# Summing products ahead of the transposes with accumulating transfers in a two-layer convolution kernel

## The reference

```python
enh  = dw_conv3x3(conv1x1(x))                      # one filter per channel
h1, h2 = split(group_conv3x3(x))
attn = conv1x1(h1 * h2) * attgamma + conv1x1(x)    # 16 values per pixel
attk = attn^T @ selfw                              # per pixel, per group of 2 channels: 2 x (2*9) weights
y    = einsum('bpgij,bpgj->bpgi', attk, uf)        # uf: the 3x3 surroundings of enh, in groups of 2 channels
out  = (y + attn^T @ selfb) * ga1 + enh + x
```

## Time and profile before

| | |
|---|---|
| median of 3 runs | 5735.58 us (5731.08 to 5740.74) |
| the profiled execution | 5731.75 us, its span 5730.0 us |
| busy in the span | PE 97%, PEld 72%, DVE 89%, ACT 60%, POOL 73% |
| layer 0 | about the first 1860 us |
| layer 1 | the rest, 64 bands |
| HBM traffic | 62 GB/s over the span |

### The profile page before, as it was taken

One profiled execution on the slowest core, in us unless ns is written; L12 is line 12 of the kernel. 1 busy time (PEld: TensorE's weight loads), 2 busy tenths in 40 slices (PEclk: granted clock), 3 DMA queues, 4 the chain that ended last, 5 costly groups with the idle time before them and its releaser, 6 DMA issues.

```text
span 5730.0 us, 115887 instructions
## 1 busy us (share of the span) xinstructions
PE 5581.3 (97%) x39944; PEld 4131.5 (72%) x39944; DVE 5083.3 (89%) x5319; ACT 3463.1 (60%) x4284; POOL 4185.7 (73%) x1831
## 2 busy tenths in 40 slices
PE   8999999999998699999999999999999999999998
PEld 7888888888886366666666766666666666766666
DVE  7888888888887789999899998989999899998989
ACT  6888888888886455455554555555455554555553
POOL 4565555555654678888888888888888888888885
PEclk9999999999999799999999999999999999999999
DMA  2222222222221222222222222222222222222221
GB/s 89 73 73 73 73 73 77 77 73 73 73 73 62 52 72 67 69 64 65 73 67 70 62 65 71 67 71 66 68 64 65 73 67 70 62 65 71 67 71 45
DMA packets 155248, 394.20 MB, mean 69 GB/s; under 512 B 35136, under 2 KB 38400, under 8 KB 155136
## 3 DMA queue, kind: packets, MB, share of 16 engines
q1 hardware_dynamic: 154800, 392.87, 22.0%
q10 hardware_dynamic: 400, 0.69, 0.1%
HBM read 219.37 MB, written 136.31 MB: 62 GB/s over the span
## 4 chain that ended last, share of the span: by engine, by line
PE 54%; DMA 8%; DVE 3%; SPq 1%; issue 1%; ACT 1%; DVEq 0%; POOLq 0%; POOL 0%; ACTq 0%
PE ps_t L888 18%; PE ps_k L871 17%; DMA xin<-layer_out 8%; PE ps_m L854 8%; PE ps_p L840 5%; PE ps_t L905 2%; DVE products L1100 2%; PE ps_t L896 1%; PE ps_t L903 1%; PE ps_m L861 1%; ACT out_sb L991 1%; SPq L736 1%; DVE products L1062 0%; SPq L684 0%; SPq L711 0%
## 5 line engine op out<-in xcount | busy, mean ns | idle before, releaser
L805 POOL TENSOR_TENSOR enh<-enh,tap 128x1280 f32<-128x1280 f32 (+1 forms) x1024 | 2512.9, 2454 | 485.2 <-ACT tap L1009 431.7
L1100 DVE TENSOR_TENSOR products<-ps_k,enh 128x1024 f32<-128x1024 f32 x1792 | 2157.4, 1221 | 269.4 <-PE ps_k L871 248.5
L871 PE MATMUL ps_k<-att,basis 128*128 128x512 f32 x4608 | 1719.3, 459 | 22.1 <-DVE products L1100 10.9
L1009 ACT ACTIVATE tap<-e,dw 128x1280 f32<-128x1280 f32 (+1 forms) x1024 | 1260.6, 1251 | 0.0
L871 PEld LDWEIGHTS ps_k<-att,basis 128*128 128x128 f32 x4608 | 719.4, 190 | 701.2 <-DVE products L1100 451.1
L296 POOL TENSOR_TENSOR hidden_lo<-hidden,hidden_hi 128x1024 fp32r<-128x1024 f32 x256 | 693.1, 2726 | 717.2 <-DVE hidden_hi L501 717.2
L888 PE MATMUL ps_t<-ident_swap,products 128*128 128x128 f32 x6144 | 921.7, 273 | 0.0
L888 PE MATMUL ps_t<-ident,products 128*128 128x128 f32 x6144 | 919.7, 272 | 0.2 <-POOL products L811 0.2
L888 PEld LDWEIGHTS ps_t<-ident,products 128*128 128x128 f32 x6144 | 757.3, 140 | 175.7 <-POOL products L811 0.5
L811 POOL TENSOR_TENSOR products<-products 128x1024 f32<-128x1024 f32 x256 | 611.8, 2390 | 268.0 <-DVE products L1100 268.0
L888 PEld LDWEIGHTS ps_t<-ident_swap,products 128*128 128x128 f32 x6144 | 719.9, 141 | 0.0
(11 more groups left out here) (111 smaller groups left out, 7378.1 us busy)
## 6 DMA issues: line engine op xcount, KB each, us to landing
xin<-layer_out SPq DMA_DIRECT2D x64, 1280.0 KB, 7.2
xt<-in_x SPq DMA_DIRECT2D x128, 512.0 KB, 4.0
layer_out<-xo SPq DMA_DIRECT2D x128, 512.0 KB, 2.9
x_own<-layer_out SPq DMA_DIRECT2D x128, 512.0 KB, 4.0
out<-out_sb SPq DMA_DIRECT2D x256, 256.0 KB, 2.0
att<-att_hi SPq DMA_DIRECT2D x512, 32.0 KB, 1.9
att<-att_lo SPq DMA_DIRECT2D x512, 32.0 KB, 2.0
h_up<-h_sb SPq DMA_DIRECT2D x256, 16.0 KB
```

The costliest lines, as they stand in the source:

```text
L805: nc.gpsimd.tensor_tensor(own, own, tap_sb[add % TAP_BUFFERS][:, 0:hi - lo, :], ALU.add).then_inc(dw_done, 1)
L871: mm = nc.tensor.matmul(ps_k[KERNEL_BUFFER[q]][:, BANK * s:BANK * (s + 1)], basis[:, 2 * t + s, :], att[p][:, j, :], start=True, stop=True)
L1009: nc.scalar.activation(tap_sb[add % TAP_BUFFERS][:, 0:hi - lo, :], src, ACT.Copy, scale=dw[:, t:t + 1]).then_inc(tap_ready, 1)
L1100: nc.vector.tensor_tensor(out, kernels, enh[p][:, r:r + CHUNK_ROWS, dx:dx + W].unsqueeze(1).to_broadcast([C, 2, CHUNK_ROWS, W]), ALU.mult) ...
```

## The change

Twelve of the 36 products were summed into their neighbours before; now it is twenty. The 28 stored products of a band make 16 terms instead of 24. The 20 sums are 8 on VectorE, 2 on GpSimd and 10 as DMA transfers with an add at the destination, which GpSimd issues: `merge_by_dma` waits for product q + 1 and adds place q + 1 to place q. Each has a semaphore of its own, for which TensorE waits ahead of the term, and VectorE before it writes the source's place again. Four sums are of three products (4+5+6, 13+14+15, 22+23+24, 31+32+33): VectorE adds the first two, a transfer the third. Terms, taps, convolution, back and the rest get other slots.

```diff
-VECTOR_MERGES = (0, 3, 10, 12, 18, 21, 27, 30)
-POOL_MERGES = (6, 15, 24, 33)
+VECTOR_MERGES = (4, 7, 13, 16, 22, 25, 31, 34)
+POOL_MERGES = (11, 29)
+DMA_MERGES = (0, 2, 5, 9, 14, 18, 20, 23, 27, 32)
+SUMMED_BEFORE = tuple(sorted(POOL_MERGES + DMA_MERGES))
-TERMS = [q for q in STORED if q - 1 not in POOL_MERGES]
+TERMS = [q for q in STORED if q - 1 not in SUMMED_BEFORE]
-TERM_SLOT = {1: 4, 2: 5, 4: 11, 5: 9, 6: 15, 8: 12, 9: 13, 11: 18, 13: 19, 14: 20, 15: 26, 17: 23, 19: 26, 20: 27, 22: 34, 23: 33, 24: 35, 26: 36, 28: 37, 29: 39, 31: 41, 32: 42, 33: 48, 35: 45}
+TERM_SLOT = {0: 10, 2: 14, 5: 15, 8: 13, 9: 21, 11: 20, 14: 27, 17: 26, 18: 34, 20: 32, 23: 35, 26: 36, 27: 40, 29: 48, 32: 49, 35: 47}
-BACK_SLOTS = [21, 30, 38, 54]
+BACK_SLOTS = [19, 28, 38, 53]
-POOL_MERGE_PLACES = (2.1, 4.5, 10.5, 13.45)
-TAP_PLACES = ((0.6000000000000001, 4.5, 5.0, 9.5, 14.5, 18.0, 18.5, 18.5, 20.5), (23.5, 25.0, 27.0, 30.0, 34.5, 35.5, 36.5, 38.5, 43.0))
-CLEAR_PLACES = (35, 53)
-H_PROD_SLOT = 27
-ATT_HIGH = 29
-ATT_LOW = 32
-CONV_SLOTS = [33, 33, 40, 40, 43, 43, 43, 43, 50, 50, 52, 52, 56, 56, 59, 59, 62, 62]
-COEFFICIENT_SLOT = 28
+POOL_MERGE_PLACES = (4.1, 13.5)
+DMA_MERGE_PLACES = (1.1, 0.5, 2.5, 3.9000000000000004, 7.5, 7.9, 8.7, 10.5, 12.4, 14.1)
+TAP_PLACES = ((0.0, 0.0, 0.0, 0.0, 6.0, 9.0, 9.5, 10.0, 11.0), (21.0, 21.5, 25.5, 27.0, 31.5, 32.0, 33.5, 35.0, 41.0))
+CLEAR_PLACES = (34, 60)
+H_PROD_SLOT = 25
+ATT_HIGH = 28
+ATT_LOW = 33
+CONV_SLOTS = [33, 33, 40, 40, 43, 43, 45, 45, 51, 51, 52, 52, 55, 55, 56, 56, 63, 63]
+COEFFICIENT_SLOT = 26
...
+                def merge_by_dma(n, index):
+                    q = DMA_MERGES[index]
+                    pool.wait_ge(product_ready, SLOTS_IN_BAND * n + OP_COUNT["product", q + 1])
+                    pool.sem_inc(dma_merge_begun, 1)
+                    nc.gpsimd.dma_start(products[:, PLACE[q], :, :], products[:, PLACE[q + 1], :, :],
+                                        accum_op=ALU.add).then_inc(dma_merged[q], 16)
...
+                    elif q in DMA_MERGES:
+                        pe.wait_ge(dma_merged[q], 16 * n + 16)
...
+                    elif at - 1 in DMA_MERGES:
+                        at_least(dve, dma_merged[at - 1], 16 * before + 16)
```

More of the change, by code:

```diff
@@ L657, in convolve @@
         pool_merged, pool_term_done = sem("pool_merged"), sem("pool_term_done")
+        dma_merge_begun = sem("dma_merge_begun")
+        dma_merged = {q: sem(f"dma_merged{q}") for q in DMA_MERGES}
         sum_done, sumT_ready, back_done, out_ready = sem("sum_done"), sem("sumT_ready"), sem("back_done"), sem("out_ready")
@@ L811, in merge @@
                     nc.gpsimd.tensor_tensor(lead, lead, products[:, PLACE[q + 1], :, :], ALU.add).then_inc(pool_merged, 1)
+                def merge_by_dma(n, index):
[4 more added lines that the diff above has]
+                                        accum_op=ALU.add).then_inc(dma_merged[q], 16)
                 ORDER = ([(t - 1, add_tap, 1, (0, t)) for t in range(1, TAPS)] +
                          [(TAPS - 1 + t - 1, add_tap, 1, (1, t)) for t in range(1, TAPS)] +
-                         [(place, merge, 2, (i,)) for i, place in enumerate(POOL_MERGE_PLACES)])
+                         [(place, merge, 2, (i,)) for i, place in enumerate(POOL_MERGE_PLACES)] +
+                         [(place, merge_by_dma, 2, (i,)) for i, place in enumerate(DMA_MERGE_PLACES)])
                 def step(items, p):
@@ L820, in step @@
                         if items[k] is not None:
-                            if action is merge:
+                            if action in (merge, merge_by_dma):
                                 action(items[k], *args)
```

## The result

The changed kernel takes 5727.19 us (median of 20 runs, 5714.12 to 5741.81), the kernel before 5740.02 us (20 runs): ratio 0.9978, 95% interval 0.9971 to 0.9985. That is 13 us less where 205 were forecast, 0.2 us a band. The profiled execution took 5723.56 us with a span of 5721.8.

A forecast was written before the change was run, and what follows sets the result against it. TensorE was taken as the bound. VectorE's 53.9 + 1.2 for late sums gave 55.1 us, GpSimd's 55.1 + 1 gave 56.1 us a band; 3.2 us less times 64 is 205 us, so 5530 us, range 5410 to 5800.

The forecast's parts named there:

- The bound before: Kernel before, convolution stage: TensorE's instruction stream bounds the 59.3 us band, VectorE 5 us behind.
- The issue: Accumulating transfer's issue in GpSimd's in-order stream: 1.1 us each, scaled from xin's 0.73, bounds 0.33 and 2.39.
- GpSimd's stream: GpSimd per band: adds 39.3 us, two merges 4.8, ten issues 11.0, together 55.1 us, more than VectorE.
- The times of the sums against TensorE's slots: Landings of transferred sums: (0,1) 1.2 us late for TensorE, (14,15) 0.9 late, (27,28) just in time.
- Other queues: SP's queue: xin's load has 7.6 us for 7.2, free unless sharing engines with an accumulating transfer, then one to three us.
- rival B: Accumulating transfers crowd the loads or land at 6 us and more: 58.5 us a band, 5680 us; chance 0.16.
- the load of h_up: From h_rows to h_prod: 7.6 us available for 5.4 us of issues, landing and h_sb, hidden with 2 us to spare.
- if the sums cost nothing: Band with fewer terms and free sums: 54.5 us, as VectorE and TensorE, coupled by two kernel buffers, won't mesh perfectly.
- TensorE's stream: Eight terms fewer a band at 0.88 us: 7.0 us less, from 58.8 to 51.8 us.
- A: Rival: GpSimd's issue is cheap, 0.5 us or less; VectorE bounds the band at 54.5 us, 5425 us; chance 0.20.
- C: Rival: an issue costs GpSimd over 1.5 us, so GpSimd paces the band; 5880 us at 1.75 us; chance 0.15.
- D: Rival: transfers each hold all DMA engines over 4.6 us and bound the band; 6290 us at 5.5 us; chance 0.09.

The follow-up runs named there:

- one attempt at it: Changed kernel with the xin load first, plus convolution moved from slots 40 and 63 to 41 and 62, product 17's term from 26 to 23: 5559.79 us.

## Why the prediction was wrong

**The bound before and the new prices were right.** The issue was forecast at 1.1 us and took 1.015; GpSimd's stream at 55.1 us a band came to about 52 (887 of 1000 us busy), mostly because an add starts 0.6 us behind an issue and only grows by some 0.35. The landing was forecast at 5 us and took 5.2, the share at 0.5 to 0.85 and came to 0.70. The times of the sums against TensorE's slots were close enough: with everything else in place (the load first), TensorE's weight loads wait 25 times in some 53 bands, 0.4 us each, and its matmuls 1.6 us in all. The Trainium skill (Collectives: The Full Stack, The bandwidth ceiling, under Why ReduceScatter is half of AllGather) states that the add in such a transfer costs time through its second source read and not in itself. The runs here agree: the transfers' own queue takes 23.4% of the engines' time in the stage when plain and 46.5% with the add.

**The step that failed is "Other queues".** It found the right place: xin's load, issued behind store(o,3), with 7.6 us for 7.2, and "one to three us a band if it does" share the engines. But the forecast then took the case in which it doesn't, and gave the other to rival B with 0.16. The same working had the engines 30 to 47 us busy in a band of 55; with a cover of 0.4 us, sharing was the rule and not the exception. The time from xin's issue to TensorE's need was as forecast, 7.6 to 7.9 us in the two bands shown (7.6); the term that was off is the landing, 9.4 us for 7.2, and the wait, 1.66 us for none. The run with the load first takes away that wait, and with it the lowered clock and the wait for h_up, and gives 5560 us; the run with an eighth of the bytes gives 5556 in the original order. Rival B was the mechanism, and its price, 58.5 us a band, was 0.6 us short of 59.07.

**What B's price left out.** No row of the kernel before had shown TensorE idle for 2.5 us in the stage, and the prediction priced a wait by its length. Behind 18 of the 25 long waits the clock fell, worth 0.6 us a band on the average. And the load of h_up, named in the prediction and put as hidden with 2 us to spare, cost VectorE 0.4 us a band (19.0 us in 50.8 bands, 18 times). B's 2 to 3 us over the forecast came out at 3.0, but mostly as these three together and not as one wait.

**A second error didn't show.** The prediction put the band at 54.5 us if the sums cost nothing; without transfers it is 56.08. TensorE's stream was put at 51.8 us, and its busy time there is 53.8 us a band (2875.86 of 3000 us), 4.8 less than before and not 7.0, with 2.3 us idle. A term does still take 0.88 us by its starts, and the modelled ends of TensorE's records reach into gaps, so how much of the difference is work and how much is gaps isn't shown. The meshing with VectorE, put at 0.6 us over 53.9, costs 2 us. By taking away one load at a time, ten issues from GpSimd or 7 us from VectorE, the band stays at 56.0 to 56.1 us; what is left as the bound is TensorE with its order of work, by exclusion. The forecast of 56.1 us came from GpSimd's sum, which doesn't bind. Had xin been in time, it would have been nearly right (56.3), by luck and for the wrong engine. Which order of TensorE's work would close the last 2 us stays open; one attempt at it gained nothing.

**The rivals.** A (cheap issue) is refuted by the 1.015 us, and its time wouldn't have come either: with plain issues of 0.56 us the kernel takes 5588 us, without any 5539, not 5425. C isn't what happened, ten issues leave GpSimd 4 us of slack; that GpSimd paces the band when its stream is long enough is shown by the halved transfers, its deciding point of 1.5 us an issue by no run. D is refuted: the ten hold the engines for 0.46 x 59.1 / 10 = 2.7 us each, not 4.6.

## What to carry to other kernels

When an edit adds traffic, take every transfer whose landing an engine meets with less than a transfer's worth of cover and price it as late; then look at what its issue is queued behind, since moving it ahead of an unrelated store was worth 167 us here, with no instruction more. Test an added mechanism in parts: the issue with few of the bytes, the bytes without the add, neither. Take away what seems to bind before calling it the bound. And price a wait of TensorE by its length and by the clock that can fall behind it.

## What the runs showed of the hardware

An accumulating transfer between two places of SBUF, 128 rows of 4 KB, takes GpSimd 1.02 us for the issue against 0.56 us for the plain one (1.07 us at an eighth of the bytes), and lands in 5.2 us against 3.3. With two issues in a row, of half the bytes each, the records overlap and are 1.54 us long on the average, 1.1 us of busy time each. The add behind an issue starts 0.6 us after the issue's start and is some 0.3 us longer behind an accumulating one. A 1280 KB load landed in 7.3 us without the transfers, in 8.3 beside plain ones and in 9.4 beside accumulating ones.

The granted clock fell to 0.54 behind a wait of 2.47 us and came back some 4 us after. In the changed kernel it fell behind 18 of the 25 waits of 2.10 to 2.89 us, the shortest of them 2.24, and behind none of the 25 of up to 1.4 us; behind 2.10, 2.44 and 2.66 us it also stayed once or more. The Trainium skill (TensorE: Matmul & The Clock Gate, Why this matters for your kernels) advises against idle gaps above some 3 us. Here gaps below that were enough in most cases, and the measurement decides.
